# A graph layer in front of a routed expert layer: counts turned one row block later, stages of the head interleaved, and a 10 MB fill of DRAM started later

## What is computed

```python
edge_index = jnp.stack([src, dst])
x = x + gnn(_layernorm(x), edge_index, W_l, b_l, W_r, gamma, beta)
x = x + ffn(_layernorm(x)[None], gate_w, ..., mlp_b2)[0]

def gnn(x, edge_index, W_l, b_l, W_r, gamma, beta):
    summed = segment_sum(x[src], dst, num_segments=n)
    cnt = segment_sum(ones(E), dst, num_segments=n)
    aggr = summed / maximum(cnt, 1.0)[:, None]
    h = aggr @ W_l.T + b_l + x @ W_r.T
    mu, var = mean(h, axis=0), mean(square(h - mu), axis=0)
    return relu((h - mu) * rsqrt(var + EPS) * gamma + beta)

def ffn(x, ...):   # 4 experts, top 2 of 4: attention (8 heads) and a gelu MLP per expert
    ...
```

## Time and profile before

| | us |
|---|---|
| median of 3 runs | 1277.0 |
| lowest, highest | 1270.0, 1277.83 |
| the profiled execution, its own time | 1274.83 |
| its span, first to last instruction | 1272.7 |
| PE busy in it | 1048.5 |
| DVE, ACT, POOL busy | 739.4, 455.5, 321.4 |

### The profile page before, as it was taken

The page is one execution under the profiler, slowest core; times in us unless marked ns, Lnnn a source line. Parts: engine busy times, 40 slices in busy tenths (PEclk is TensorE's granted clock), DMA queues, the critical chain, the costliest instruction groups (busy, mean ns, idle before and its releaser), DMA issues.

```text
span 1272.7 us, 19546 instructions
## 1 busy us (share of the span) xinstructions
PE 1048.5 (82%) x5155; PEld 568.0 (45%) x5156; DVE 739.4 (58%) x1609; ACT 455.5 (36%) x850; POOL 321.4 (25%) x300
## 2 busy tenths in 40 slices
PE   1986789999946878688776989799897999889974
PEld 1654567778623433334343434344343335433333
DVE  5385543452384678547864574756748248646753
ACT  1301112222433553436525334434344532336521
POOL 3102233453438535114420030000000133313211
PEclk9987789998967989899897989999999999989997
DMA  5193000000356515201503020000003121210010
GB/s 154 40 271 105 1 2 0 0 0 1 108 165 197 141 36 194 81 1 53 179 26 121 1 67 1 1 0 0 0 0 100 34 66 46 77 39 1 2 32 35
DMA packets 34830, 75.64 MB, mean 59 GB/s; under 512 B 8203, under 2 KB 8501, under 8 KB 34474
## 3 DMA queue, kind: packets, MB, share of 16 engines
q1 hardware_dynamic: 26122, 55.91, 14.3%
q0 software_dynamic: 8320, 16.49, 4.4%
q10 hardware_dynamic: 288, 2.10, 0.5%
HBM read 49.06 MB, written 26.70 MB: 60 GB/s over the span
## 4 chain that ended last, share of the span: by engine, by line
PE 65%; DVE 15%; issue 9%; ACT 5%; POOL 2%; DMA 1%; DVEq 1%; SPq 1%; ACTq 0%; POOLq 0%
PE bank L1422 16%; PE bank L1513 9%; PE bank L1270 9%; PE bank L1309 5%; PE bank L1543 4%; PE bank L1598 3%; DVE den L2264 3%; PE bank L1477 2%; PE bank L1305 2%; PE bank L1498 2%; PE bank L1500 2%; PE bank L1237 2%; DVE oT L2266 1%; PE bank L1557 1%; PE bank L1292 1%
## 5 line engine op out<-in xcount | busy, mean ns | idle before, releaser
L1875 DVE TENSOR_SCALAR oh_src<-iota,edge 125x1250 f16 x178 | 101.2, 568 | 107.2 <-PE bank L1270 101.7
L1513 PE MATMUL bank<-probs_t,v_head 128*128 128x512 f32 (+1 forms) x288 | 147.1, 594 | 7.0 <-ACT probs_t L1055 6.4
L1055 ACT ACTIVATE probs_t<-bank 128x512 f32<-128x512 f32 x144 | 81.5, 573 | 136.0 <-PE bank L1500 135.4
L2177 DVE TENSOR_REDUCE mx<-bank 128x1 f32<-128x512 f32 x144 | 88.5, 656 | 63.9 <-PE bank L1477 63.0
L1270 PE MATMUL bank<-oh_src,oh_dst 125*125 x534 | 112.1, 362 | 2.9 <-DVE oh_dst L1877 0.8
L590 POOL TENSOR_TENSOR w<-w_stage,w 128x1024 f16<-128x1024 f32 x35 | 75.5, 2167 | 132.9 <-ACT w L857 132.8
L1598 PE MATMUL bank<-probs_t,v_head 128*128 128x128 f32 (+2 forms) x192 | 88.0, 545 | 6.9 <-ACT probs_t L1106 5.1
L1270 PEld LDWEIGHTS bank<-oh_src,oh_dst 125*125 x534 | 71.2, 144 | 43.9 <-issue 24.9
L1422 PE MATMUL bank<-hT,w 128*128 128x256 f16 (+1 forms) x552 | 89.1, 325 | 1.5 <-DVE hT L2109 1.5
L1543 PE MATMUL bank<-hT,w 128*128 128x512 f16 x288 | 72.5, 385 | 7.7 <-ACT t L1080 7.7
L1422 PE MATMUL bank<-w,hT 128*128 128x512 f16 x264 | 67.0, 408 | 8.9 <-DVE hT L2109 8.9
(11 more groups left out here) (323 smaller groups left out, 1945.4 us busy)
## 6 DMA issues: line engine op xcount, KB each, us to landing
w_stage<-in_ew_dram SPq DMA_DIRECT2D x40, 512.0 KB, 4.4
lists<-zeros SPq DMA_DIRECT2D x1, 10340.0 KB
x_in<-lists SPq DMA_DIRECT2D x15, 517.0 KB, 5.8
x_mem<-lists SPq DMA_DIRECT2D x3, 1024.0 KB, 5.3
x_mem<-lists SPq DMA_DIRECT2D x1, 2560.0 KB, 10.0
out_dram<-x_mem SPq DMA_DIRECT2D x10, 250.0 KB
table<-rows SPq DMA_DIRECT2D x5, 449.8 KB
big<-in_x_dram SPq DMA_DIRECT2D x10, 224.0 KB
```

The lines of the kernel that those rows point to most:

```text
L1055: nc.scalar.activation(probs_t[:, x % NPB, 0:cn], stb[x % 2][:, 0:cn], ACT.Exp).then_inc(s_exp, 1)
L1513: nc.tensor.matmul(pvb[(hd * nq + s) % 2][:, 0:cn], v_head[:, hd, kt, :], probs_t[:, (hd * nx + i) % NPB, 0:cn], start=(k == 0), stop=(k = ...
L1875: nc.vector.tensor_scalar(oh_src[:, bass.ds(slot, 1), i, 0:N].rearrange("p a n -> p (a n)"), iota[:, :], edge[:, 0, i, bass.ds(g, 1)], Non ...
L2177: nc.vector.tensor_reduce(mx[:, hd, t, s:s + 1], sbk[i % 2][:, 0:cn], AX.X, ALU.max).then_inc(s_mx, 1)
```

## The change

1. **Head, DVE:** the x tiles come first; the edges are converted while POOL computes 1/std of the first half; the statistics and the normalisation of the second half, the group bounds (`meetings`) and the gate halves are placed between the steps of the projection.
2. **Head, PE:** the transposes for the edges and the gate's means come between the projections of later tiles, and the wait for `w_lo` stands only before the last four matmuls of `project_y(0)`.
3. **Head, POOL and ACT:** `w_lo` of the first matrix is made before the powers; the load of the second matrix is issued when the first has been rounded.
4. **Counting:** `turn_rows(0)` comes after `count_rows(1)`, `turn_rows(1)` after `count_rows(2)` and before `combine(0, 0)` (in a branch of the loop, taken for b = 1), and in `combine` the wait for `at_lo` comes after the first 12 matmuls.
5. **Fill:** SP waits for the third scaling (`s_ascale` 3) before it issues the zeros.

```diff
@@ SP
             sp.wait_ge(s_const, 7)
+            sp.wait_ge(s_ascale, 3)
             sp.dma_start(lists.rearrange("(i p) d -> p i d", p=P),
@@ POOL
+            low_message(0)
             for half_t in range(2):
                 ...
                 nc.gpsimd.tensor_tensor(rstd[0:TT, tiles], mv[0:TT, tiles, 1], half[0:TT, tiles],
                                         ALU.pow).then_inc(s_rstd, 1)
-            for m in range(2):
-                pool.wait_ge(s_whi, m + 1)
-                nc.gpsimd.tensor_tensor(w_lo[:, m, :, :], w_r[:, m, :, :], w_hi[:, m, :, :],
-                                        ALU.subtract).then_inc(s_wlo, 1)
+            low_message(1)
@@ ACT
-            act.dma_start(w_r[:, 1, :, :].rearrange("p c n -> p (c n)"), gnn_w[:, KC * D:2 * KC * D]).then_inc(s_gw1, 16)
 ...
             nc.scalar.copy(w_hi[:, 0, :, :], w_r[:, 0, :, :]).then_inc(s_whi, 1)
+            act.dma_start(w_r[:, 1, :, :].rearrange("p c n -> p (c n)"), gnn_w[:, KC * D:2 * KC * D]).then_inc(s_gw1, 16)
@@ PE
                 for k, (a, w) in enumerate([(xnT_hi, w_hi), (xnT_lo, w_hi), (xnT_hi, w_lo)]):
+                    if k == 2 and t == 0:
+                        pe.wait_ge(s_wlo, 1)
 ...
             for t in range(NT + 1):
                 if t < NT:
                     turn_x(t)
-                if t == 1:
-                    pe.wait_ge(s_wlo, 1)
                 if t >= 1:
                     project_y(t - 1)
+                if t == 5:
+                    turn_edges()
+                    gate_means()
+                if t == 7:
+                    turn_meeting()
+                if t == 9:
+                    turn_bounds()
 ...
             def combine(b, u):
-                pe.wait_ge(s_atlo, b * 6 + 9)
                 for i in range(2):
 ...
+                    if i == 0:
+                        pe.wait_ge(s_atlo, b * 6 + 9)
                     for k, (w, a) in enumerate([(y_hi, at_hi), (y_lo, at_hi), (y_hi, at_lo)]):
 ...
             with nc.tensor.Fori(0, 2) as t:
                 count_rows(t)
-                turn_rows(t)
+            turn_rows(0)
             with nc.tensor.Fori(1, NB) as b:
                 for u in range(2):
                     count_rows(b * 2 + u)
+                    if u == 0:
+                        with nc.tensor.If(b < 2):
+                            turn_rows(1)
                     combine(b - 1, u)
                     turn_rows(b * 2 + u)
@@ DVE (the edge work, row_moments and normalise that stood ahead of the loop are now in it)
+            for t in range(NB):
+                row_stats(t)
+            row_moments(0)
+            dve.wait_ge(s_edges, 32)
+            nc.vector.tensor_copy(edge[:, :, :, 0:NG], edge_i[:, :, :, :]).then_inc(s_edge, 1)
+            normalise(0)
             for t in range(NT + 1):
                 if t < NT:
                     low_x(t)
                 if t >= 1:
                     low_y(t - 1)
+                if t == 0:
+                    row_stats(NB)
+                    row_stats(NB + 1)
+                if t == 1:
+                    for k in range(NB + 2, NT):
+                        row_stats(k)
+                if t == 2:
+                    row_moments(1)
+                if t == 3:
+                    normalise(1)
+                if t == 6:
+                    meetings()
+                if t == 7:
+                    gate_halves()
+                if t == 8:
+                    dve.wait_ge(s_turnmeet, 1)
+                    nc.vector.tensor_reduce(meet_c[:, :], banks[1][0:2 * NT, 0:NG], AX.X, ALU.max).then_inc(s_meetc, 1)
+            dve.wait_ge(s_turnmeet, 2)
+            (the two writes of meets)
```

More of the change, by code:

```diff
@@ L612, in _, with low_message @@
             nc.gpsimd.memset(zeros[:, :], 0.0).then_inc(s_const, 1)
+            def low_message(m):
+                pool.wait_ge(s_whi, m + 1)
+                nc.gpsimd.tensor_tensor(w_lo[:, m, :, :], w_r[:, m, :, :], w_hi[:, m, :, :],
+                                        ALU.subtract).then_inc(s_wlo, 1)
+            low_message(0)
             for half_t in range(2):
@@ L1202, in _, with turn_edges, turn_meeting, turn_bounds @@
         def _(pe):
[L1204 to L1219, removed]
+            def turn_edges():
+                pe.wait_ge(s_edge, 1)
+                for i in range(G):
+                    last = nc.tensor.transpose(banks[0][0:NG, i * TT:(i + 1) * TT], edge[:, 1, i, 0:NG],
+                                               ident[0:TT, 0:TT])
+                last.then_inc(s_edgeT, 1)
+            def turn_meeting():
+                pe.wait_ge(s_meetv, 1)
+                nc.tensor.transpose(banks[1][0:2 * NT, 0:NG], meet_v[:, :, :].rearrange("p k t -> p (k t)"),
+                                    ident[0:NG, 0:NG]).then_inc(s_turnmeet, 1)
+            def turn_bounds():
+                pe.wait_ge(s_meetc, 1)
+                nc.tensor.transpose(banks[2][0:1, 0:2 * NT], meet_c[:, :],
+                                    ident[0:2 * NT, 0:2 * NT]).then_inc(s_turnmeet, 1)
+            def gate_means():
+                pe.wait_ge(s_gate, 32)
+                for c in range(KC):
+                    last = nc.tensor.matmul(banks[5][:, 0:NE], mean_d[:, :], gate_t[:, c, :], start=(c == 0),
+                                            stop=(c == KC - 1))
+                last.then_inc(s_gmean, 1)
             def turn_x(t):
@@ L1239, in project_y @@
                 last.then_inc(s_y1, 1)
+            pe.wait_ge(s_id, 1)
             for t in range(NT + 1):
@@ L1785, in link, with row_stats @@
                 dve.wait_ge(s_dch, chain[0])
[L1787 to L1802, removed]
+            def row_stats(t):
+                dve.wait_ge(s_x[t // 2], 64)
+                nc.vector.bn_stats(st6[0:TT, t, :], xn[:, t, :]).then_inc(s_st, 1)
             def row_moments(half_t):
                 tiles = slice(half_t * NB, (half_t + 1) * NB)
-                for t in range(half_t * NB, (half_t + 1) * NB):
-                    dve.wait_ge(s_x[t // 2], 64)
-                    nc.vector.bn_stats(st6[0:TT, t, :], xn[:, t, :]).then_inc(s_st, 1)
                 for t in range(half_t * NB, (half_t + 1) * NB):
@@ L1819, in normalise @@
                                             ALU.subtract, ALU.mult).then_inc(s_xn, 1)
[L1821 to L1837, removed]
@@ L1838, in _, with meetings @@
-            nc.vector.tensor_tensor(std_x[:, :], mv[0:TT, :, 1], rstd[0:TT, :], ALU.mult)
+            def meetings():
+                dve.wait_ge(s_edgeT, 1)
+                seen = banks[0][0:NG, 0:G * TT]
+                nc.vector.tensor_reduce(reach[:, 0:1], seen, AX.X, ALU.max).then_inc(s_reach, 1)
+                nc.vector.tensor_reduce(reach[:, 1:2], seen, AX.X, ALU.min).then_inc(s_reach, 1)
+                dve.wait_ge(s_const, 3)
+                dve.wait_ge(s_reach, 2)
+                nc.vector.tensor_scalar(meet_f[:, 0, :], tile_lo[:, :], reach[:, 0:1], None, ALU.is_le)
+                link(nc.vector.tensor_scalar(meet_f[:, 1, :], tile_lo[:, :], float(TT - 1), reach[:, 1:2], ALU.add,
+                                             ALU.is_ge))
+                nc.vector.scalar_tensor_tensor(meet_v[:, 0, :], meet_f[:, 0, :], g_down[:, 0:1], meet_f[:, 1, :],
+                                               ALU.mult, ALU.mult)
+                link(nc.vector.scalar_tensor_tensor(meet_v[:, 1, :], meet_f[:, 0, :], g_up[:, 0:1], meet_f[:, 1, :],
+                                                    ALU.mult, ALU.mult))
+                dve.sem_inc(s_meetv, 1)
@@ new lines, in gate_halves @@
+            def gate_halves():
+                dve.wait_ge(s_gmean, 1)
+                link(nc.vector.tensor_tensor(gate_c[:, :, :], gate_t[:, :, :],
+                                             banks[5][:, 0:NE].unsqueeze(1).broadcast_to([P, KC, NE]), ALU.subtract))
+                link(nc.vector.tensor_copy(gate_16[:, :, 0, :], gate_c[:, :, :]))
+                nc.vector.tensor_tensor(gate_16[:, :, 1, :], gate_c[:, :, :], gate_16[:, :, 0, :],
+                                        ALU.subtract).then_inc(s_gate16, 1)
+                nc.vector.tensor_tensor(std_x[:, :], mv[0:TT, :, 1], rstd[0:TT, :], ALU.mult)
@@ L1856, in _ @@
                     low_y(t - 1)
+                if t == 0:
[16 more added lines that the diff above has]
+            dve.wait_ge(s_turnmeet, 2)
+            nc.vector.tensor_scalar(meets[:, 0, :], banks[2][0:1, 0:NT], -1.0, float(NG), ALU.mult,
+                                    ALU.add).then_inc(s_meets, 1)
+            nc.vector.tensor_copy(meets[:, 1, :], banks[2][0:1, NT:2 * NT]).then_inc(s_meets, 1)
             dve.sem_inc(s_ohused, RING)
```

## The result

The changed kernel is slower. Its median is 1289.14 us (4 runs, 1286.24 to 1293.04) against 1275.26 for the kernel before; the ratio is 1.0118, with a 95% interval of 1.0093 to 1.0144. The forecast was 1255, with a range of 1247 to 1265. The profiled execution has a span of 1284.3 us against 1272.7.

The account below looks back on a forecast made before the run. The prediction took PE, busy 1048.5 of 1272.7 us, as the bound, with waits on other engines early on. Head 10.8 plus counting 10.3 less 0.4 for the skipped branch, 20.7 us off 1274.83, gave 1254, stated as 1255 (1247 to 1265).

Parts of the forecast that it names:

- The step that failed: From tile 3 to the layer's end: PE bounds unchanged code, so gains before about 175 us carry through one for one.
- Rival (c): Counting loop: every pass stops for its code, 4.3 us a stop, 26 us at tiles 4 to 9, giving 1280; chance 0.05.
- The fill: Zero fill moved from the count of tile 0 to tile 2's scaling: 0, within 2 us either way.
- Rival (d): Counting, first pass: the fill's new place doubles the two stops, 2.59 + 3.05 us more, giving 1260; chance 0.05.
- Head: Start and projection: 14.4 us earlier start, less 3.2 and 0.4 us coming back, gives 10.8 us (5 to 13).
- the term of 2.8 us: Head: x lands earlier because the second matrix no longer goes ahead; 2.8 us taken, bounds 0 and 3.6.
- What came back in the loop: Projection: work moved between its steps costs 3.2 us (1.5 to 8.5), and later writes of `meets` 0.4.
- Counting: Tiles 0 to 2: moving the transposes later hides waits for POOL's scaling, gaining 10.3 us (6 to 13).
- The rule of the two locks: Counting, tiles 1 and 2: POOL's scaling could hold DVE 3.5 us twice; taken as 0, without cover 1262.
- The sum itself: Whole kernel: 10.8 + 10.3 - 0.4 = 20.7 us gained, giving 1254, stated as 1255.

Follow-up runs that it names:

- e4: The changed kernel with the transposes of tile 1 moved out of PE's counting loop, ahead of it; ratio 1.0111 to the kernel before.
- e16: The changed kernel with 232 semaphore increments on PE ahead of the counting (120 and 112); ratio 1.0000 to the kernel before.
- e9: The kernel before with only the fill's wait for the third scaling added; median 1280.7 us, ratio 1.0064.
- e10: The changed kernel with PE's counting written out for 10 groups in the loop over the blocks and the fill at its old place; 1254.55 us, ratio 0.985.
- e11: The changed kernel with PE's counting written out for 10 groups in the loop over the blocks, keeping the fill's wait; 1260.76 us, ratio 0.9886.
- e13: The changed head with the counting order of the kernel before and the fill at its old place; 1264.66 us, ratio 0.9925.
- e12: The kernel before with PE's counting written out for 10 groups in the loop over the blocks; 1269.97 us, ratio 0.9973.
- e14: The kernel before with 25 semaphore increments at the start of PE's program, where it stands idle; 1305.67 us, ratio 1.021.
- e15: The kernel before with 256 semaphore increments on PE ahead of the counting (70 and 186); 1300.26 us, ratio 1.0204.
- e1: The changed kernel with all of PE's counting code written out for 10 groups instead of 16; 1270.51 us, ratio 0.9954 to the kernel before.
- e7: The changed kernel with 120 semaphore increments at the start of PE's program and 136 where it waits for the routing; ratio 1.0447 to the kernel before.
- e6: The kernel before with 25 semaphore increments at the start of PE's program and 231 where it waits for the routing; 1323.81 us, ratio 1.0387.

## Why the prediction was wrong

- **The step that failed** is the one that ended "So what is won or lost before about 175 us moves all that follows one for one", with its ground, "The code behind tile 3 is not changed". The text of the code was not, its place was. Rival (c) named the effect, priced a stop at 4.3 us and put the sum at 1280; it got 0.05, because "the body grows by little". The size of the growth was the wrong question, since 18 places without any growth (e4) do the same. In its place the runs showed 33 us lost in tiles 3 to 9, 23 of them more time standing still and 10 at the lower clock, and of the 33 some 5 to 8 belong to the next point. With the loop at a good place (e16) there are no late stops.
- **The fill** was put at 0 in its new place. It costs 8 us in e9 (1.0064) and 4.6 between e10 and e11. I had taken the price of a stop beside the fill from the end of tile 0: 2.77 us against 2.59 and 3.05 without. That row was misread: the stop lasts from 106.23 to 109.00, and the fill was running out just then. The DMA queues moved 275 GB/s from 106 to 107 us, 130 and 23 in the two microseconds after; the window's row of the kernel before:

```profile
106.00:111.00 5.00, 0.44 (x3) 0.13 (x1) 4.24 (x14) 1.33 (x3) 0.22 (x1) 0.99 0.25 86
```

  With the fill at full rate for the whole stop, at the end of tile 3, it is 7.84 (e9), 9.32 (changed) or 7.74 us (e11). Rival (d) had this with 5.6 us and 0.05.
- **Head: right in mechanism, 1.9 us too large.** Forecast 10.8 us, measured 8.9 at the first count matmul, and 9.6 by the ratio of e13. The landing of x did not come earlier: 6.97 + 9.01 = 15.98 against 15.80. Taking 1 MB of the other queue away changed nothing, so the term of 2.8 us was 0. What came back in the loop was close: the projection starts 11.4 us earlier and the counting 8.9, so 2.5 us came back where 3.6 were forecast. The stall of 4273 ns is gone, all ten normalisations take 536 to 546 ns.
- **Counting: right.** Forecast 10.3 us; in the changed kernel the lead grows from 8.9 to 18.6 at tile 2, 9.7 us. The fill of tile 1 waits for ACT 1.91, that of tile 2 3.22 (about 3.7 forecast) and `at_lo` costs 0.78 (0.6 uncovered in the forecast).
- **The rule of the two locks** (the Trainium skill, SBUF — State Buffer, Who interferes with whom: VectorE in a two-port mode and GpSimd lock each other out for a whole instruction) fits what is seen, and the delay was covered as assumed. The longest one-hot, from 126.25 us on beside POOL's scaling of 125.57 to 129.05, is now 3145 ns instead of 1243 (first fence: the line's durations, min/median/max), and PE waited for one-hots 0.8 us in all (second fence: the page's row of the count):

```profile
L1915 DVE TENSOR_SCALAR oh_src<-iota,edge x178: 529/541/3145, 60.4 to 308.2; 125x1250 f16 x178
```

```profile
L1289 PE MATMUL bank<-oh_src,oh_dst 125*125 x534 | 116.0, 368 | 3.6 <-DVE oh_dst L1917 0.8
```

- **The sum itself** was near, and the match of the number is partly luck. e10, the changed order without late stops and with the fill at its old place, takes 1254.55 us, where 1255 was forecast for the fill at its new one. Of its 19 us some 3 belong to the short body (e12: 0.9973). That leaves about 16 us, give or take 4, for head and counting, where 20.7 were forecast.

## What to carry to other kernels

A long loop on PE can have a price that no instruction in it shows: count its instructions in the built program and note where it starts and ends in pieces of 256, since 25 instructions that do nothing, *ahead* of the loop, cost some 27 us here (e14) and 256 cost nothing but their own time (e15). When a profile shows "issue" stops inside a loop that had none, compare the packets of the instruction queue before looking for a wait. A cheap test is to shift the loop by a known number of places. A large transfer that nobody waits for can still cost time: here a stop of PE for code took 4.4 to 6 us longer beside it, so keep it away from the first passes of a loop.

## What was not expected of the hardware

- A stop for code in the first pass costs PE 2.6 to 3.3 us with idle queues in the kernel before, e13 and e15 (2.3 to 4.9 over all runs, without e1), and 7.4 to 9.3 us at the end of tile 3 beside a transfer at some 200 to 330 GB/s. The stop at the end of tile 0 is 2.7 us with the fill running out beside it and 2.73 us without any fill (e9).
- A shift by 25 places makes the kernel before 27 us slower by the ratio; a shift by 256 leaves its loop without late stops, as it was. The Trainium skill (Runtime: NRT & Kernel Launch, Instruction fetch mechanics) gives 16 KiB blocks of 256 instructions and room for 2048 on PE; the packets of 16.4 KB and the period of 256 agree. A body of 1875 places would fit in 2048 by that rule wherever it spans 8 blocks; that this alone is enough is what e7 speaks against, as worked out above.
- A semaphore increment on PE took 0.11 to 0.13 us in a row (136 in 14.4 us in e7, 231 in 29.1 us in e6, 186 in 24 us in e15).
